# Four edits to a four-layer transformer kernel: order of the opening transfers, activation tables, merge rows 8 partitions apart, and one copy ahead of the router's exps

## The reference

```python
mod = (silu(L_c) @ L_wmod).reshape(16, 6, 1, -1)
sa, ca, ga, sb, cb, gb = ...                      # ga, gb: at least 0.25 in size
h = layernorm(x) * (1 + ca) + sa;  x = x + ga * attention(h)
h = layernorm(x) * (1 + cb) + sb;  x = x + gb * feed_forward(h)
```

```python
# layer 2
g   = (relu(h @ gate_w1.T + gate_b1) @ gate_w2.T + gate_b2).mean(axis=1)   # (16, 8)
mW1 = W1 + einsum('be,efh->bfh', g, TW1);  mb1 = b1 + g @ Tb1              # 512 x 128 and 512
mW2 = W2 + einsum('be,ehf->bhf', g, TW2);  mb2 = b2 + g @ Tb2              # 128 x 512 and 128
out = gelu(h @ mW1.T + mb1) @ mW2.T + mb2
# layer 3
w, idx = top_k(softmax(h @ router_w), 6)
out = sum_k w_k * (silu(h @ g_k) * (h @ u_k)) @ d_k  +  (silu(h @ gs) * (h @ us)) @ ds
```

## Time and profile before

| what | value |
|---|---|
| median of 3 runs | 2697.95 us (2694.12 to 2698.86) |
| the profiled execution's own time | 2697.07 us |
| its span, first to last instruction | 2695.2 us |
| PE busy | 2488.2 us, 92% |
| DVE busy | 1883.5 us, 70% |
| ACT busy | 1461.8 us, 54% |
| POOL busy | 645.8 us, 24% |
| mean granted TensorE clock | 0.969 |

### The profile page before, as it was taken

How to read it: one execution, slowest core, us unless ns; L and a number is a source line. 1 busy time by engine, 2 the same in 40 slices (tenths; PEclk the granted TensorE clock), 3 DMA queues, 4 the chain that set the end, 5 groups by cost and what they waited for, 6 DMA issues and landing times. The chain is left out here.

```text
span 2695.2 us, 61799 instructions
## 1 busy us (share of the span) xinstructions
PE 2488.2 (92%) x19656; PEld 2049.2 (76%) x19656; DVE 1883.5 (70%) x5964; ACT 1461.8 (54%) x4035; POOL 645.8 (24%) x1166
## 2 busy tenths in 40 slices
PE   6999999998999999999998999969998677999888
PEld 5788888887888798999997888846665465666666
DVE  5777777776667487888887766656775245777687
ACT  5888888886444355665555322324555243455544
POOL 0000000001111000110001110146773035777322
PEclk9999999999999899999999999979998788999999
DMA  3200000002000355555553000066553936555100
GB/s 121 34 1 1 0 0 0 1 1 67 1 1 1 119 158 156 171 169 165 167 164 102 1 1 0 1 192 162 150 150 78 208 74 157 151 151 151 29 15 16
DMA packets 196812, 221.53 MB, mean 82 GB/s; under 512 B 12900, under 2 KB 180212, under 8 KB 195076
## 3 DMA queue, kind: packets, MB, share of 16 engines
q1 hardware_dynamic: 196612, 219.11, 29.0%
HBM read 118.42 MB, written 100.12 MB: 81 GB/s over the span
## 5 line engine op out<-in xcount | busy, mean ns | idle before, releaser
L890 DVE TENSOR_REDUCE a_nmax<-bank 128x2 f32<-128x512 f32 x256 | 164.8, 686 | 147.8 <-PE bank L825 147.8
L1463 ACT ACTIVATE a_p<-a_p,a_nmax 128x256 f32<-128x256 f32 x256 | 128.3, 502 | 209.1 <-DVE a_nmax L1664 209.1
L313 POOL TENSOR_TENSOR delta<-y,arena 128x256 f32<-128x256 f32 x30 | 23.1, 772 | 850.8 <-ACT y L306 850.8
L2176 ACT ACTIVATE a_p<-bank 128x1024 f32<-128x1024 f32 (+1 forms) x256 | 193.4, 808 | 21.1 <-PE bank L2236 16.8
L1767 ACT ACTIVATE f_silu<-bank 128x512 f32<-128x512 f32 x128 | 76.7, 599 | 205.2 <-PE bank L153 204.6
L2116 POOL TENSOR_SCALAR_AFFINE_SELECT a_p<-a_p 128x512 f32<-128x512 f32 x256 | 163.6, 639 | 0.0
L2394 DVE TENSOR_REDUCE a_nmax<-bank 128x4 f32<-128x1024 f32 x128 | 155.4, 1214 | 3.5 <-PE bank L2223 3.5
L1144 ACT ACTIVATE f_hidden<-bank,arena 128x512 f32<-128x512 f32 x128 | 87.7, 686 | 127.1 <-PE bank L153 127.0
L1218 PEld LDWEIGHTS bank<-arena,f_hidden 128*128 128x128 f32 x1024 | 135.1, 193 | 22.6 <-issue 4.5
L1218 PE MATMUL bank<-arena,f_hidden 128*128 128x128 f32 x1024 | 144.6, 281 | 6.8 <-DVE f_acc L1285 3.0
L734 ACT CAST a_qk<-bank 128x256 fp32r<-128x256 f32 x256 | 95.1, 371 | 91.1 <-PE bank L153 91.1
(11 more groups left out here) (376 smaller groups left out, 7764.4 us busy)
## 6 DMA issues: line engine op xcount, KB each, us to landing
pos_dram<-a_pos SPq DMA_DIRECT2D x128, 383.0 KB, 2.9
a_stack<-rows_dram SPq DMA_DIRECT2D x128, 320.0 KB, 4.1
rows_dram<-a_cut SPq DMA_DIRECT2D x192, 192.0 KB, 2.5
a_shifted<-pos_dram SPq DMA_DIRECT2D x128, 256.0 KB, 2.7
merged_dram<-f_staged SPq DMA_DIRECT2D x16, 578.0 KB, 8.7
f_merged<-merged_dram SPq DMA_DIRECT2D x16, 578.0 KB, 10.2
gate<-gates_dram SPq DMA_DIRECT2D x32, 256.0 KB, 11.2
arena<-in_task SPq DMA_DIRECT2D x4, 1156.0 KB, 7.7
```

The costliest lines, as they stand in the source:

```text
L890: dve.tensor_reduce(nmax[:, at.ring(2), h, :], s_ps[h][:].rearrange("p (t k) -> p t k", t=NT), AX_X, ALU.max, negate=True).then_inc(s["nma ...
L1463: i = act.activation(p[:, at.ring(4), t, :], p[:, at.ring(4), t, :], ACT.Exp, bias=nmax[:, r, t:t + 1], accum_out=sums[:, r, t:t + 1])
L2176: act.activation(p[:, b4.ring(2), first:end], sT_ps[:, first:end], ACT.Exp).then_inc(s["exp"], 1)
```

## The change

Seven places are edited.

- In the prologue SP issues the later layers' `wmod` directly behind the first sequences of `x`, then `wq0`, `wk0`, `wv0` (with a semaphore of their own, `qkv_in`, for which ACT's rounding waits now), the mask, `wo0`, `bo0`, and the other sequences last. PE waits for that `wmod` before its transposes, and makes the modulations of layers 1, 2 and 3 before, between and behind the two transposes.
- `load_table` is new: an activation of one number per partition into an unused tensor. It stands at the start of attention 0 (Exp), behind the late square root of both `rope_attention` stages (Exp) and of `ffn3` (Tanh), and in `ffn2` between the last gate activation and `stage(9)` (Gelu).
- In `ffn2` the task vectors' rows are laid out so that merge `r` of a half gives the weight rows `r, r+8, ..., r+120`, not `16r ... 16r+15`; its place writes every eighth partition. Bytes, numbers of transfers and instructions stay.
- In `ffn3` ACT copies `partsT` ahead of the two exps.

```diff
+def load_table(act, k, function):
+    act.activation(k.unused[:], k.ident[:, 0:1], function)
...
-                for g in range(NB // FIRST):
+                def load_x(g):
...
+                load_x(0)
+                sp.dma_start(wmod[:, 1:4], d["wmod"][:, 1:4]).then_inc(sems["mod_in1"], 16)
+                for piece in range(QKV_PIECES):
+                    load_weight_piece(sp, k, d, 0, piece, opening.qkv_in)
+                sp.dma_start(opening.maskf[:], d["causal"]).then_inc(opening.mask_in, 16)
+                for piece in range(QKV_PIECES, weight_pieces(0)):
+                    load_weight_piece(sp, k, d, 0, piece)
+                for g in range(1, NB // FIRST):
+                    load_x(g)
...
-                act.wait_ge(k.weights_in[0], 16 * weight_pieces(0))
+                act.wait_ge(opening.qkv_in, 16 * QKV_PIECES)
...
+                pe.wait_ge(sems["mod_in1"], 16)
                 pe.wait_ge(sems["ident_in"], 16)
                 for j in range(2):
+                    of_layer(1 + j)
                     pe.wait_ge(sems["xn"], j + 1)
...
-                pe.wait_ge(sems["mod_in1"], 16)
-                for layer in range(1, 4):
-                    mm = of_layer(layer)
-                mm.then_inc(sems["mod_mm"], 1)
+                of_layer(3).then_inc(sems["mod_mm"], 1)
...
+                load_table(act, k, ACT.Exp)          # attention0, start; both rope_attention stages, step 1
...
-                    sp.dma_start(merged[ROWS * r:ROWS * (r + 1), HALF * half:HALF * (half + 1), :],
+                    sp.dma_start(merged[r:P:GROUPS, HALF * half:HALF * (half + 1), :],
...
+                load_table(act, k, ACT.Gelu_apprx_tanh)
                 for j in range(GROUPS + 1, GROUPS + EARLY_MERGES, 2):
                     stage(act.copy, act, j)
...
+                    if at.p == 4 and ni.real:
+                        wait(act, s["partsT_mm"], ni, item=True)
+                        wait(act, s["share_mm"], at, 2, item=True)
+                        act.copy(partsT[:], partsT_ps).then_inc(s["partsT"], 1)
                     if at.p == 4 and i2.real:
...
-                    if at.p == 4 and ni.real:
-                        wait(act, s["partsT_mm"], ni, item=True)
-                        wait(act, s["share_mm"], at, 2, item=True)
-                        act.copy(partsT[:], partsT_ps).then_inc(s["partsT"], 1)
...
+                        load_table(act, k, ACT.Tanh)
...
-    o["task"] = task.reshape(8, 8, 16, -1).transpose(0, 2, 1, 3).reshape(P, 8, -1)
+    o["task"] = task.reshape(P, 8, -1)
```

More of the change, by code:

```diff
@@ L407 @@
 FIRST = 4
+QKV_PIECES = 3
 class Opening:
@@ L423, in __init__ @@
         self.mask_in = ctx.enter_context(nc.semaphore("mask_in"))
+        self.qkv_in = ctx.enter_context(nc.semaphore("qkv_in"))
 def rounded_piece(k, i):
@@ L467, in _ @@
                                  ).then_inc(opening.x_in[g], 16)
-                    if g == 0:
-                        load_weights(sp, nc, k, d, 0)
-                        sp.dma_start(wmod[:, 1:4], d["wmod"][:, 1:4]).then_inc(sems["mod_in1"], 16)
-                        sp.dma_start(opening.maskf[:], d["causal"]).then_inc(opening.mask_in, 16)
+                load_x(0)
[7 more added lines that the diff above has]
+                    load_x(g)
             @block.gpsimd
@@ L587, in weight_pieces, with load_weight_piece @@
     return sum(PIECES.get(name, 1) for name, _, _ in WEIGHTS[phase])
-def load_weight_piece(sp, k, d, phase, piece):
+def load_weight_piece(sp, k, d, phase, piece, landed=None):
     at = 0
@@ L600, in load_weight_piece @@
             sp.dma_start(k.arena[phase % 2][0:parts, at + piece * part:at + (piece + 1) * part], whole
-                         ).then_inc(k.weights_in[phase], 16)
+                         ).then_inc(landed or k.weights_in[phase], 16)
         piece -= cuts
@@ L710, in step @@
                     if at.number(10):
+                        pool.wait_ge(k.weights_in[phase], 16 * (weight_pieces(phase) - QKV_PIECES))
                         pool.wait_ge(k.gate_in[phase], 16 * GATE_PIECES)
@@ L794, in _ @@
                 pe.sem_inc(s["ht_mm"], 2)
+                pe.wait_ge(k.weights_in[phase], 16 * (weight_pieces(phase) - QKV_PIECES))
                 def step(at):
@@ L967, in build @@
         k.spare = ctx.enter_context(nc.sbuf_tensor("spare", [1, 1], F32))[:]
+        k.unused = ctx.enter_context(nc.sbuf_tensor("unused", [P, 1], F32))
         k.mod = ctx.enter_context(nc.sbuf_tensor("mod", [P, 8, 2, NB], F32))
@@ L2179, in step @@
                         late_std(act, k, s)
+                        load_table(act, k, ACT.Exp)
                     if at.number(END - 14):
```

## The result

| | median | runs | ratio to before, 95% interval |
|---|---|---|---|
| before | 2696.03 us | 2690.95 to 2698.86 (4) | |
| changed | 2650.28 us | 2643.31 to 2657.43 (4) | 0.9833 [0.9801, 0.9864] |
| changed, two further series | 2658.51 and 2655.47 us | 2646.29 to 2663.55 (10) | 0.9837 [0.9809, 0.9864], 0.9846 [0.9828, 0.9865] |

Forecast were 2656.9 us, a ratio of 0.985. The profiled execution of the changed kernel took 2643.31 us, with a span of 2641.5: 53.7 us less than the profiled one of before. That is more than the medians differ by (45.7, and 40.1 and 44.5 in the later series), so each stage has to be judged by its own stretch of the profile. To cut the span I use ACT's table loads for the square root (line 188 in all kernels) and the one behind it, which stand at fixed places of a stage.

A forecast was written before the change was run, and what follows sets the result against it. The DMA queue was taken to bound `ffn2`, and waits for `partsT` to cost time in `ffn3`. Terms 22.6 + 12.6 + 3.2 + 1.25 + 0.8 - 0.2 = 40.2 us, from 2697.07, gave 2656.9 us; range 2641 to 2675.

The forecast's parts named there:

- the likeliest case: Whole kernel: the forecast itself, 2656.9 us, with its own range 2643 to 2668 us and chance 0.76.
- What bounds `ffn2`: In `ffn2` the DMA queue bounds: busy 91% from 2083 to 2140.7 us, while DVE works 12 of 57.7 us.
- The saving per place: In `ffn2` each place to rows 8 apart saves half of its 4.1 us, 2.05 us; bounds no saving and 2.7.
- half of 4.1: In `ffn2`, the saving taken for one place of 4.1 us of queue time: 2.05 us.
- Places about 3.5 us apart: In `ffn2`, a sign: issues of place(2) to place(7) come about 3.5 us apart instead of 5.56.
- The number of places on the path: In `ffn2`, 7 places before add_base(0) and about 4 around out(15) and place(15): 11 x 2.05 = 22.6 us.
- `partsT`: In `ffn3`, copying it ahead of the exps saves 1.05 us per lap in 12 laps, 12.6 us; laps of 8.85 us.
- Opening: In the prologue, reordered transfers land `wmod` at 10.7 us and end the stage at 22.9 for 26.1: 3.2 us saved.
- Tables: Early table loads gain 1.25 us in attention 0, 0.8 in `ffn2`, 0 in both `rope_attention` stages, and -0.2 in `ffn3`.
- Places that stay slow: Rival in `ffn2`: places don't get quicker, so the 22.6 us go and the time is 2679.5 us; chance 0.08.
- an `ffn3` bound by DVE: Rival: `ffn3` stays because DVE bounds it, gaining 3 us in place of 12.6, for 2666.5 us; chance 0.12.
- slower scattered rows: Rival in `ffn2`: a place to scattered rows takes twice as long, 8.2 us, for 2724.5 us; chance 0.04.

The follow-up runs named there:

- rows 2 apart: The changed kernel with a merge's 16 rows 2 partitions apart, within 32 neighbouring ones, instead of 8 apart over all 128: 2657.82 us, ratio 0.9836.
- no tables: The changed kernel without its four early table loads, every other part in: 2661.27 us, ratio 0.9855.

## Why the prediction was right, step by step

The time (2650 to 2659 us in three series) lies within the likeliest case's own range. By stage, averaged over profiled executions that share an edit and over those that don't:

| term | predicted | by stage | alone, by the runs |
|---|---|---|---|
| rows 8 apart, with the table in `ffn2` | 22.6 + 0.8 | 185.1 - 157.8 = 27.3 | 24.3 |
| `partsT` first, with the table in `ffn3` | 12.6 - 0.2 | 150.0 - 137.8 = 12.2 | 10.5 |
| opening and table in attention 0 | 3.2 + 1.25 | 663.3 - 659.5 = 3.8 | 5.9 (opening only) |
| sum | 40.2 | 43.3 | |

(For `ffn2`: before and the three kernels with neighbouring rows; the changed kernel's three executions, rows 8 apart alone, rows 2 apart, and no tables. `ffn3`: the four kernels with the old order, the ten with the new one. The start: the four kernels with the old opening, the ten with the new one.)

The three parts alone and the tables' 1.0016 multiply to 0.9865, where the whole gave 0.9833 to 0.9846: within their intervals.

- **What bounds `ffn2`.** Right. The queue is full before and after in the first half (0.91), and stage(7), add_base(0) and add_base(8) all come earlier once places are shorter.
- **The saving per place.** The forecast 2.05 us is about what a cycle saved on average, by luck: "half of 4.1" was a middle between two bounds, and the 4.1 us come from the quickest of four profiles. From place(2) to place(6) a cycle shrank by 5.65 - 3.96 = 1.69 us between the profile of before and the first of the changed kernel, and by 5.99 - 3.98 = 2.01 over all profiles of the table's row. "Places about 3.5 us apart" was wrong: 5.56 less 2.05, but they came 3.96 apart.
- **The number of places on the path.** Too small: 11. `ffn2` gained 27.3 us on average, 13.6 times the 2.01. Up to add_base(0) the average gain is 16.1 us, eight times the saving, where 7 places gave 14: 1.9 from place(0) to place(2), 9.0 from there to place(7), 4.7 between place(7)'s issue and add_base(0), and 0.5 before any place is issued, which is chance. In the second half the sum had 4 places at 2.05, 8.2. The stretch from out(15)'s issue to add_base(8) shrank from 18.7 us in the profile of before (20.8 to 21.1 in the three others with neighbouring rows) to 9.3 to 9.5, 11.1 on average. There the backlog, not only the place, is gone: nothing is left ahead of out(15), which lands in 3.8 us for 9.3, as out(0) does with an empty queue (3.9 in the same profile), and place(15) in 5.4 for 9.3. Between the profile of before and the first of the changed kernel the errors have opposite signs: a saving of 1.69 for 2.05, and 25.7 us of gain for 22.6.
- **`partsT`.** The mechanism and the length of a lap were right: 12 laps from 2508.39 to 2614.60 us are 8.85 each. Before, the same twelve were 9.74 on average and not the 9.90 of the earlier trace rows, which I read in one lap from the middle. That is 0.89 and not 1.05 per lap, in 13 laps and not 12; the last two laps are as long as before (8.6 and 8.0 us). PE, not DVE, bounds the stage now: it is busy 95% of it, DVE 85%.
- **Opening.** `wmod` at 10.7, DVE as the last engine and ACT's copies at 21.2 were forecast; measured 10.8, DVE last, 20.5. The first cast of attention 0 comes at 27.3 to 27.8 us in the four profiles with the old opening and at 23.1 to 24.6 in the ten with the new one, 3.5 us sooner on average. That the kernel with that edit alone shows 3.2, as the sum has it, is chance within 1.5 us.
- **Tables.** The load in attention 0 does leave the path of the first exp: from the first cast it takes 6.4 to 7.0 us with the load in front and 5.4 to 5.7 without, 1.2 on average. Whether the stage's end, 600 us later, keeps any of it isn't shown: with the new opening the stage ends at 657.2 to 662.4 us with early loads and at 660.1 and 660.4 without. In `ffn2` the 0.8 us can't be read from PE's wait for the first Gelu, as I had done; this wait is as long now (0.82 us for 0.80 in the earlier trace rows), though no load is in front:

```profile
2111.71 1.22 PE L2659 MATMUL bank<-f_merged,f_uT 128*128 128x128 f32 x4 [0.82 <-ACT f_uT L2568]
```

What holds ACT there now is stage(11), whose copy comes later against the main loop than before. ACT's timeline in the changed kernel, then in the one without tables:

```profile
2110.16 1.12 ACT L2498 COPY f_staged<-bank 128x1156 f32<-128x1156 f32 x1 [7.86 <-DMA merged_dram<-f_staged]
```

```profile
2128.43 1.12 ACT L2496 COPY f_staged<-bank 128x1156 f32<-128x1156 f32 x1 [7.41 <-DMA merged_dram<-f_staged]
2129.57 1.28 ACT L2565 ACT_TABLE_LOAD   x1
```

With rows apart, PE's first `y` matmul starts 5.2 us behind add_base(0) without the early load and 4.0 to 4.3 with it; with neighbouring rows, 4.1 to 4.3 without and 3.3 with it. So the load was worth about 1 us at that point, and the stage's length (157.2 without, 156.9 to 157.5 with) doesn't show it.

- **The rivals.** Places that stay slow, an `ffn3` bound by DVE, and slower scattered rows are each excluded by the run with that part alone: a cycle of 3.99 us for 5.65, and an `ffn3` that is 11.9 us shorter.

## What to carry to other kernels

A transfer into few neighbouring partitions can be made shorter by spreading its rows (here by some 40%), with no change in bytes or instructions; it takes only a new order of the weights on the way in. Where a full queue is relieved, count every transfer in it, the first and the last too; the last gain more than their own saving, since the backlog ahead of them goes. One profile gives one sample: the cycle that I read as 5.6 us was 6.0 to 6.2 in three others. Before bytes are taken out of a queue by cutting transfers up, multiply the number of issues by the time of one: here eight small ones cost more than the detour over memory. And a copy that is ready should not stand on an engine behind work that waits.

## What the runs showed of the hardware

- For 16 rows of 37 KB the busy DMA engines together move 225 GB/s in a mix of outs and places if the rows are neighbours and 305 if they are 2 or 8 apart. With two transfers of 8 rows it is 406, but at a share of 0.66.
- The packet of one row of 36,992 bytes, in a transfer of 16 rows, took 3.70 to 4.13 us on average into neighbouring partitions (four profiles) and 2.36 to 2.44 into every eighth or every second (six); in transfers of 8 rows, 4 apart, 1.37 (median). For a whole place the estimates are 144 and 237 GB/s (592,000 bytes in 4.1 and 2.50 us).
- Two transfers of 8 rows issued one behind the other were served one behind the other, eight rows at a time.
- The issue of a transfer from tile to tile of 16 rows takes SP 0.59 us (median of 128), where an out or a place to neighbouring rows takes 0.32 and a place to every eighth row 0.48. ACT takes 0.67 (four in 2.68).
- The activation behind a table load starts 1.29 us after the load's start (22.25 and 23.54; 30.32 and 31.61), so nothing is lost but the 1.28 us of the row itself. In the profile of before 28 of the 33 loads behind ACT's first instruction are like this, and 30 of them start 0.02 us behind the end of what ran ahead. The drain of about 1.38 us that the Trainium skill adds (ScalarE: Activation LUTs, "What ACT_TABLE_LOAD costs") is not seen in these rows.
- The same program's untouched 1050 us differ by up to 15 us from one profiled execution to the next. A part worth 2 us can't be judged from two profiles' spans.
